# The first attention tile by gathered rows instead of matmuls, its additions spread over the tail

## What is computed

```python
idx = _knn(x_loc, k)                         # k = 30 neighbours
# relative coordinates -> angles -> three small layers with batch norm -> h
att = jax.nn.softmax(h[..., 0], axis=-1)     # 30 weights for each point
xk = x.transpose(0, 2, 1)[bidx, idx]         # the 30 neighbours' rows
agg = jnp.einsum('bnkc,bnk->bnc', xk, att)
return x + agg.transpose(0, 2, 1)
```

## Time and profile before

| what | value |
|---|---|
| median of 3 runs | 702.93 us |
| lowest and highest | 702.05 and 703.98 us |
| the profiled execution | 704.21 us |
| its span in the trace | 702.4 us |
| mean granted TensorE clock | 0.995 of full |

### The profile page before, as it was taken

How to read it: one execution, slowest core, us unless ns; L and a number is a source line. 1 busy time by engine, 2 the same in 40 slices (tenths; PEclk the granted TensorE clock), 3 DMA queues, 4 the chain that set the end, 5 groups by cost and what they waited for, 6 DMA issues and landing times.

```text
span 702.4 us, 13067 instructions
## 1 busy us (share of the span) xinstructions
PE 684.0 (97%) x5388; PEld 578.4 (82%) x5388; DVE 578.8 (82%) x848; ACT 345.5 (49%) x529; POOL 354.8 (51%) x294
## 2 busy tenths in 40 slices
PE   5999999999999999999999999999999999999998
PEld 4799889878888888788888988987987877888887
DVE  5699999999799899966689998777886998678831
ACT  6456547348525227857793355483472443233210
POOL 2268767664867877400039667657679850000000
PEclk9999999999999999989999999999999999999999
DMA  9520300200000022744422712513624740101001
GB/s 349 192 4 1 119 1 5 87 28 3 1 2 0 2 65 87 244 154 161 157 99 91 120 75 81 100 71 95 105 76 120 115 66 2 46 31 47 32 32 60
DMA packets 35932, 54.94 MB, mean 78 GB/s; under 512 B 15392, under 2 KB 15648, under 8 KB 35872
## 3 DMA queue, kind: packets, MB, share of 16 engines
q1 hardware_dynamic: 29136, 42.51, 17.8%
q0 software_dynamic: 6208, 10.54, 9.3%
q10 hardware_dynamic: 528, 1.05, 0.4%
HBM read 40.06 MB, written 12.73 MB: 75 GB/s over the span
## 4 chain that ended last, share of the span: by engine, by line
PE 81%; DVE 8%; POOL 4%; issue 3%; ACT 3%; DMA 1%; SPq 0%; POOLq 0%; ACTq 0%
PE bank L1620 25%; PE bank L1644 7%; PE bank L1646 6%; PE bank L1645 6%; PE bank L1682 4%; PE bank L1744 4%; PE bank L1785 4%; PE bank L1787 4%; PE bank L1530 4%; PE bank L1786 4%; PE bank L1532 4%; PE bank L1531 4%; DVE idx L1108 2%; DVE vals L1106 2%; POOL p_second L572 1%
## 5 line engine op out<-in xcount | busy, mean ns | idle before, releaser
L1620 PE MATMUL bank<-nbr,pts_h 128*128 128x512 f32 (+2 forms) x512 | 193.9, 381 | 2.4 <-DVE pts_l L1136 1.5
L1620 PE MATMUL bank<-nbr,pts_l 128*128 128x512 f32 (+2 forms) x512 | 191.2, 376 | 0.0
L572 POOL TENSOR_TENSOR p_second<-p_first,p_second 128x512 f32<-128x512 f32 x58 | 76.6, 1324 | 99.3 <-ACT p_second L838 99.3
L1620 PEld LDWEIGHTS bank<-nbr,pts_h 128*128 128x128 f32 x512 | 97.2, 190 | 20.0 <-POOL pts_l L583 2.5
L1620 PEld LDWEIGHTS bank<-nbr,pts_l 128*128 128x128 f32 x512 | 97.2, 190 | 15.0 <-issue 0.2
L852 ACT CAST pts_h<-bank 128x512 fp32r<-128x512 f32 (+2 forms) x64 | 35.1, 554 | 144.9 <-PE bank L1620 144.7
L1644 PE MATMUL bank<-wT,pts_h 128*128 128x512 f32 x256 | 102.1, 399 | 0.1
L1646 PE MATMUL bank<-wT,pts_l 128*128 128x512 f32 x256 | 100.0, 391 | 0.0
L1645 PE MATMUL bank<-wT,pts_h 128*128 128x512 f32 x256 | 99.9, 390 | 0.0
L583 POOL TENSOR_TENSOR pts_l<-p_second,pts_h 128x512 fp32r<-128x512 f32 x58 | 79.5, 1376 | 3.1 <-ACT pts_h L844 2.0
L1530 PE MATMUL bank<-pts_h 128*128 128x512 f32 (+3 forms) x192 | 69.2, 360 | 8.0 <-DVE pts_l L1068 7.5
(11 more groups left out here) (222 smaller groups left out, 1448.5 us busy)
## 6 DMA issues: line engine op xcount, KB each, us to landing
p_rows<-p_second SPq DMA_DIRECT2D x32, 256.0 KB, 2.0
more<-a_rows SPq DMA_DIRECT2D x16, 480.0 KB, 4.6
scratch<-a_rows SPq DMA_DIRECT2D x14, 480.0 KB, 5.1
X<-in_ctx SPq DMA_DIRECT2D x12, 512.0 KB, 6.3
out_dram<-X SPq DMA_DIRECT2D x15, 256.0 KB, 2.0
more<-in_ctx SPq DMA_DIRECT2D x4, 512.0 KB, 5.8
X<-in_x SPq DMA_DIRECT2D x2, 1024.0 KB, 6.4
X<-in_x SPq DMA_DIRECT2D x1, 1536.0 KB, 6.9
```

The source lines that it names most:

```text
L572: pool.tensor_tensor(p, a, b, ALU.subtract).then_inc(s_p32, 1)
L1620: mm = pe.matmul(bank[u % 3][:, 0:w], p[:, m, t * P:(t + 1) * P], nbr[b][:, m, hf * HALF:hf * HALF + w], start=(m == 0 and part_ == 0), st ...
```

## The change

Tile 0 is no longer attended by matmuls. SP stores the final X of batch 0 to DRAM (`x_d`, 8 stores of 256 KB, behind all stores of p). VectorE keeps tile 0's indices and weights (`idx_first`, `w_first`), since their places are used again. GpSimd gathers, for each of the 30 neighbour slots, the 128 rows of X of that slot into 12 buffers in turn (4 in `more`, 8 in `w_raw`, free after the last projection), and VectorE adds each row times its weight to X's tile 0 in place (`add_row`). `ROWS_BESIDE` says how many are added beside each tile: 1, 3, 3 in tiles 1 to 3, 1 each in tiles 9 to 11, 6 each in tiles 12 to 14, 2 in tile 15. `attend` runs over tiles 1 to 15, counts and waits are lowered by one, and tile 0 is stored ahead of the last tile only. In tiles 1 to 3 the one pair of spread groups stands ahead of the sixth row group instead of the second.

```diff
+            for m in range(NT):
+                sp.wait_ge(s_xu, NT * (ITS - 2) + m + 1)
+                sp.dma_start(x_d[m * P:(m + 1) * P, :], X[:, 0, m, :]).then_inc(s_xd, 16)
-            for T in range(TILES):
+            for T in (*range(1, TILES - 1), 0, TILES - 1):
...
-                    sp.wait_ge(s_fo, T + 1 + (cols.start > 0))
+                    if T:
+                        sp.wait_ge(s_fo, T + (cols.start > 0))
+                    else:
+                        sp.wait_ge(s_add1, K1)
...
+        row_of = sums + [w_raw[:, i // CT, i % CT, :] for i in range(2 * CT)]
...
+            for k in range(K1):
+                if k == 0:
+                    pool.wait_ge(s_xd, 16 * NT)
+                    pool.wait_ge(s_gt, tiles_gathered(ITS))
+                if k == len(sums):
+                    pool.wait_ge(s_wm, NT * ITS)
+                if k >= len(row_of):
+                    pool.wait_ge(s_add1, k - len(row_of) + 1)
+                pool.indirect_dma_start(out=row_of[k % len(row_of)], out_offset=None, in_=x_d,
+                                        in_offset=bass.IndirectOffsetOnAxis(ap=idx_first[:, k:k + 1], axis=0)) \
+                    .then_inc(s_row[k % len(row_of)], 16)
...
+                link(dve.tensor_scalar(idx_first[:], idx[:, 0, :], 0, None, ALU.logical_shift_right))
+                link(dve.tensor_copy(w_first[:], att32[:, 0, :]))
                 link(dve.tensor_scalar(idx_last[:], idx[:, TILES - 2:TILES, 0:K0], 0, None, ALU.logical_shift_right))
...
+            ROWS_BESIDE = (0, 1, 3, 3, 0, 0, 0, 0, 0, 1, 1, 1, 6, 6, 6, 2)
+
+            def add_row(k):
+                dst = X[:, 0, 0, :]
+                dve.wait_ge(s_row[k % len(row_of)], 16 * (k // len(row_of) + 1))
+                if k:
+                    dve.wait_ge(s_add1, k)
+                dve.scalar_tensor_tensor(dst, row_of[k % len(row_of)], w_first[:, k:k + 1], dst, ALU.mult, ALU.add).then_inc(s_add1, 1)
...
-                if i < AB and len(tail_groups(i)) <= 3:
+                if 1 < i < AB and len(tail_groups(i)) <= 3:
                     xT_low(AB + i)
+                if i == 1:
+
+                    xT_low(AB)
+                    xT_low(AB + 1)
...
                 for r in range(AB):
-                    if r % 4 == 1:
-                        for q in beside[r // 2:r // 2 + 2]:
-                            spread(q)
+
+                    for q in {1: beside[:2] if len(beside) > 2 else (), 5: beside[-2:]}.get(r, ()):
+                        spread(q)
...
-            for i in range(CHUNKS * CT):
+            for i in range(1, TILES):
                 attend(i)
```

More of the change, by code:

```diff
@@ L100, in build @@
         idx = sb("idx", [P, TILES, KP], U32)
+        idx_first = sb("idx_first", [P, KP], U32)
+        w_first = sb("w_first", [P, KP], F32)
         idx_last = sb("idx_last", [P, 2, K0], U32)
@@ L116, in build @@
         tab_d = nc.dram_tensor("table", [N, 3], F32, kind="Internal").ap()
+        x_d = nc.dram_tensor("x_rows", [N, C], F32, kind="Internal").ap()
         a_rows = nc.dram_tensor("a_rows", [CHUNKS, P, P], BF16, kind="Internal").ap()
@@ L278, in build @@
         s_join = sem("sums_joined")
+        s_xd = sem("x_rows_stored")
+        s_row = [sem(f"neighbour_rows_landed{i}") for i in range(len(row_of))]
+        s_add1 = sem("neighbour_rows_added")
         s_gt = sem("gathered_q_turned")
@@ L974, in spread_out @@
                 elif q % NG == 0:
-                    act.wait_ge(s_f, CH * (c - 1))
+                    act.wait_ge(s_f, CH * (c - 1) - 1)
                 act.copy(att_flat[c % 2].rearrange("p (x n) -> p x n", n=P)[:, :, (q % NG) * GN:(q % NG + 1) * GN],
@@ L1463, in result @@
                 dst = X[:, i // NT, i % NT, :]
-                dve.wait_ge(s_f, i + 1)
+                dve.wait_ge(s_f, i)
                 if i < TILES - 1:
@@ L1469, in result @@
                     cols = slice(hf * C // 2, (hf + 1) * C // 2)
-                    dve.wait_ge(s_f, TILES + hf)
+                    dve.wait_ge(s_f, TILES - 1 + hf)
                     dve.tensor_tensor(dst[:, cols], bank[(0, 3)[hf]][:, cols], dst[:, cols], ALU.add).then_inc(s_fo, 1)
+            ROWS_BESIDE = (0, 1, 3, 3, 0, 0, 0, 0, 0, 1, 1, 1, 6, 6, 6, 2)
[5 more added lines that the diff above has]
+                dve.scalar_tensor_tensor(dst, row_of[k % len(row_of)], w_first[:, k:k + 1], dst, ALU.mult, ALU.add).then_inc(s_add1, 1)
             xT_low(AB - 1)
@@ L1477, in _ @@
                         onehots(q // 2)
-                    if n == 1 and i:
+                    if n == 1 and i > 1:
                         result(i - 1)
@@ L1481, in _ @@
                         xT_low(AB + i)
-                if i and len(tail_groups(i)) <= 1:
+                if i > 1 and len(tail_groups(i)) <= 1:
                     result(i - 1)
-                if i < AB and len(tail_groups(i)) <= 3:
+                if 1 < i < AB and len(tail_groups(i)) <= 3:
                     xT_low(AB + i)
+                if i == 1:
+                    xT_low(AB)
+                    xT_low(AB + 1)
+                done = sum(ROWS_BESIDE[:i])
+                for k in range(done, done + ROWS_BESIDE[i]):
+                    add_row(k)
             result(CHUNKS * CT - 1)
@@ L1768, in attend @@
                 c, t, b = i // CH, i % CH, i // NT
-                if t == 0:
+                if t == 0 or i == 1:
                     pe.wait_ge(s_scc, NG * (c + 1))
                     pe.wait_ge(s_xTl, NT * (b + 1))
-                if i >= 3:
-                    pe.wait_ge(s_fo, i - 2)
+                if i >= 4:
+                    pe.wait_ge(s_fo, i - 3)
                 beside = list(tail_groups(i))
```

## The result

| what | before | after |
|---|---|---|
| median of 20 runs | 704.18 us | 700.06 us |
| ratio after to before | | 0.9956, 95% interval 0.9944 to 0.9969 |
| the profiled execution | 704.21 us | 703.56 us |
| its span | 702.4 us | 701.8 us |
| tail: from the first attention matmul to the end of the span | 110.59 us | 107.70 us |

The change gives 0.44%, 3.1 us (2.2 to 3.9). The medians are 4.1 us apart, the means, 703.6 and 700.7, only 3.0, without one execution of 708.67 us in a slower state, which the ratio leaves out too. Forecast were 4.84 us, 0.69%. 704.18 us less 3.1 is 701.1, above the upper end of the range, 700.7; that the median after, 700.06, lies inside it is no merit of the forecast, as the executions fall into two groups, and the median stands in the faster one, which holds a few more.

A forecast was written before the change was run, and what follows sets the result against it. The tail was taken as a chain of TensorE work alone; -5.44 us for tile 0's matmuls and +0.6 for two small copies gave -4.84, from the median of 702.93 to 698.1 us, range 697.0 to 700.7.

The forecast's parts named there:

- 24 matmuls, -5.44 us: Tail on TensorE: leaving out tile 0's 24 matmuls of 512 columns takes 5.44 us off the path.
- Two small copies, +0.6 (0 to 1.1): VectorE's index chain ahead of the tail: two chained copies lengthen the path by 0.6 us, between 0 and 1.1.
- rival 2: Ahead of the tail nothing is lost, as the small copies fit into GpSimd's busy time: 697.5 us; chance 0.15.
- X stores against p gathers, 0 (up to 2): Ahead of the tail, X stores share DMA engines with the first p gathers: 0 us lost, at most 2.
- Rival 1: Last iteration's gathers held up 2 to 4 us, TensorE waits at 572, 1 to 3 us lost: say 700; chance 0.10.
- Row price 0.73: VectorE in the tail: each of 30 dependent row additions takes 0.73 us, 21.9 us in all, within idle time.
- the slack ahead of tile 4: VectorE's one-hot set for tile 4's first spread is done at 611.1, wanted at 611.95: 0.9 us to spare.
- Rival 3: Gather issues block VectorE's row additions in the tail, 11.1 us late: 709.2 us, slower than before; chance 0.06.
- rival 4: Last gathers land late, rows 27 to 29 hold VectorE at the half results: 699 to 704, say 701; chance 0.05.
- all hidden in tiles 1 to 3, no wait of TensorE in the tail: VectorE's added work in tiles 1 to 3 fits its idle time; TensorE never waits in the tail: 0 us.
- at tile 2, 3 or 4: Sign that would prove the forecast wrong: TensorE waiting for one-hots at one of these tiles; no size given.
- The base: Time the sum was taken off: median of three runs, 702.93 us; the profiled execution was 704.21.

The follow-up runs named there:

- first profile: Profiled execution of the changed kernel in the first comparison with the kernel before, no further edit: 703.56 us, tail 107.70 us.
- late-rows kernel: Changed kernel with no row additions in tiles 1 to 3, the seven rows added in later tiles: ratio to the kernel before 0.9929, on another chip 0.9932.
- extra traffic: Changed kernel with 16 more 256 KB DRAM-to-DRAM copies issued by SP behind the output stores of tiles 1 to 4: ratio to the kernel before 0.9969.
- spaced gathers: Changed kernel with gathers 13 to 19 issued singly behind the results of tiles 4 to 10: ratio to the kernel before 0.9934, on another chip 0.9949.
- held kernel: Changed kernel with gathers held until the results of tiles 3 and 4, and no row addition before tile 5: ratio to the kernel before 0.9933.

## Why the prediction was right and wrong

- **24 matmuls, -5.44 us**: right. 110.59 to 105.15 us with nothing but tile 0 gone, 105.2 with rows and gathers in an undisturbed execution.
- **Two small copies, +0.6 (0 to 1.1)**: the chain was delayed by half a microsecond (0.49 at the iota, counted from the chain's start), near the forecast, but not as it was made up: the copies took 0.54 and 1.22, the one behind them 1.21 instead of 0.53, and the 128x512 operation 0.43 instead of 1.47. Wrong was that it stays: it was absorbed at 577, in the same idle time that the prediction had used to excuse the X stores. Measured 0.4, zero not excluded; rival 2 described it better.
- **X stores against p gathers, 0 (up to 2)**: about right. Waits of 0.4 to 0.75 us for the turned sum appear in some profiles, but also in the two without X stores (0.41 in each), and with only the copies the wait at 577 is gone in turn. Rival 1 didn't happen.
- **Row price 0.73**: an addition takes 0.75 us, and where one waits for another the next starts after 0.85; only the last of a chain is followed after 0.67. Six rows and a result cost 5.54 rather than 5.0, seven rows in tiles 1 to 3 cost 5.4 rather than 5.1, and the slack ahead of tile 4 was 0.68, not 0.9. It hid nonetheless. Rival 3's mechanism (additions blocked by gather issues) didn't happen at all: additions beside gathers take the same 0.75. In an undisturbed execution no engine waited for any of this; where reports were late, the 0.2 us less of slack added to the loss.
- **Gathers landing late, rival 4**: no. VectorE never waited for a row.
- **The step that failed** is "all hidden in tiles 1 to 3, no wait of TensorE in the tail". The prediction priced the gathers on GpSimd, in landing time and against VectorE, and treated TensorE's reports to ScalarE and VectorE as free. In four of six comparisons they come up to 4.3 us late beside back-to-back gathers; a slack of 0.68 us can't take that. The first profile shows the price, 2.15 us of waiting of TensorE (0.75 of its own and 1.40 for VectorE's late set), and 17 of 38 executions are 2.7 us slower than the others. The sum, -4.84, is what the other half shows (-5.0), in part by luck: the copies' +0.6 wasn't there. The wait "at tile 2, 3 or 4" had been named as the sign that would prove it wrong, without a rival or a price for it.
- **The base**: three runs gave a median of 702.93, twenty 704.18. This moved the microseconds and not the percentage.

The Trainium skill, "SBUF — State Buffer", section "Who interferes with whom", says of the engines' SBUF ports that "PE and ACT never wait on anyone". That can't be carried over to TensorE's reports: here its updates were up to 4.3 us behind its matmuls beside gather issues (605.7 to 610.0), and it idled 0.75 us itself. Whether a port has a part in that no run here shows. The Trainium skill's page "Perfetto Trace Analysis", section "Tensor Engine Instruction (MATMUL, LD_WEIGHTS)", says that a matmul's end in the profile is an estimate, and that the update goes out only when PSUM has acknowledged the writes. So the row of a matmul that looks done doesn't show that its report left, and the start of whoever waits for it has to be read instead.

What stays open: why the comparisons differ, what exactly holds TensorE's update (in the pairs of the late-rows kernel it comes 0.2 to 0.4 us after GpSimd's second issue ends, in the first profile's stall in the middle of an issue, at 608.44), and why the stall at tile 2 comes in some executions and not in others of one kernel on one chip. The extra traffic beside gathers made it more frequent (all five at 0.995 instead of one of four, one chip), which only suggests that it takes part.

No version beat the changed one where it is undisturbed (0.9921 to 0.9934 for all of them). Where it isn't, later rows or spaced gathers are 1.7 to 2.1 us faster in two comparisons (0.9932 against 0.9962, 0.9949 against 0.9973, with intervals that overlap), and the held kernel is equal in a third (0.9933 against 0.9927). All three keep pairs or rows of gathers at tile 11, which cost their profiled executions 0.4 to 0.6 us at tile 12; the changed kernel's have no such wait.

## What to carry to other kernels

Work moved to idle engines is free only as far as the slack of everybody who waits at its side; where it issues gathers in a row from GpSimd, leave slack for whoever waits for TensorE there (2 to 4 us by the delays seen here), or issue them singly, behind events that are spaced anyway. Count a chained VectorE operation by the start of the next one, not by its length. And where a time is spread in clusters, take more profiles before explaining the first one: the first showed an event that only some executions have, and a comparison on another chip gave 4.8 us instead of 3.1.

## What the runs showed of the hardware

- TensorE's semaphore updates came up to 4.3 us behind the end of their matmuls (5.3 with extra traffic) while GpSimd issued gathers one after the other, and while those of VectorE and ScalarE were on time. Beside a pair of gathers 0.30 us apart it was 1.9 us, beside a single gather at most 0.4, beside none at most 0.1. Of 66 groups beside rows of gathers 29 were over 0.6 us late. Four comparisons showed it, two didn't, with the same changed kernel in all; the five behind the first ran on five chips.
- 256 KB copies issued by SP at up to 211 GB/s over 10 us, with no gathers, delayed nothing.
- A 128x512 scalar_tensor_tensor with two SBUF inputs takes 0.75 us beside gather issues and without them; a chained pair starts 0.85 apart, an unchained follower 0.67 behind.
- After TensorE had idled 1.6 us in all between 602.9 and 605, its granted clock fell to half from 605.3 on for 3.4 us (extra traffic's kernel, a mean of 0.67 from 604 to 608). After 0.75 us of idle time in the first profile it stayed at full.
